# Weights of six stages of a four-layer network, requested during the normalisation ahead of each stage

## The chip, the cores and the metric

The kernel runs on one core of one Trainium2 chip. Its time is that of one execution on the device, in microseconds (us): the median of three runs was 2194.48 us (2192.84 to 2197.96). Before it is compared with after on the same measure.

## What is computed

The input is `x`, 2 sequences of 1024 tokens with 128 features, all float32. Four layers follow one another; each adds two residual branches, and each branch begins with a layer normalisation without scale or shift:

```python
x = x + L0_attn(layernorm(x))   # 16 heads of 64, causal softmax, two graph steps on the attention matrix, a linear map, projection, layernorm
x = x + L0_ffn(layernorm(x))    # 128 -> 512, a sine transform of the hidden values, relu, 512 -> 128
x = x + L1_attn(layernorm(x))   # one head of 64, causal softmax, projection
x = x + L1_ffn(layernorm(x))    # 8 experts of 128 x 128, each token takes the output of one
x = x + L2_attn(layernorm(x))   # 16 heads of 8, linear attention, gated
x = x + L2_ffn(layernorm(x))    # 8 experts, two per token, with a capacity
x = x + L3_attn(layernorm(x))   # state-space mixer: projection, convolution, scan over 16 states, projection
x = x + L3_ffn(layernorm(x))    # 8 experts, one per token
```

## The kernel before, in words

`x` stays in on-chip memory for the whole program, as `main_x` of 128 partitions by 16 tiles by 128 features. The program is a sequence of stages. Each stage opens a `scope` (lines 83 to 103), which hands out on-chip buffers, accumulator banks and semaphores, and then one block with a program for each engine. When a scope is left, GpSimd clears the scope's semaphores and all engines meet in a barrier (L89 in the profile). So no engine passes from one stage to the next before the slowest has ended its part, and a stage's buffers are free for the next stage.

Ahead of every branch stands `prenorm` (lines 106 to 169), a stage of its own. VectorE takes mean and variance of the 16 token tiles (L57, L60), ScalarE the square root (L145), VectorE five small steps and 16 normalised tiles `n_xn` (L132), TensorE turns each of them (L162), and ScalarE copies the turned tiles into `main_xnT`, 512 columns at a time (L148). The first layer runs this twice over (`rounds=2`). The last ScalarE copy ends the stage. SyncE has nothing to do in it, except where a router stands behind it: then the router's own small constants are requested there (L121).

Six branches request their weights at the start of their own stage, behind the barrier. SyncE issues the requests one after another, and the engines wait for a semaphore that counts all of them:

- `l0_attention` (prefix `l0a`): 13 requests of constants and masks (L302 to L309), eight of which wait until GpSimd has cleared three matrices (L331), since two blocks of 64 x 64 are put on the diagonal of each; then the first pair of heads' weights `wp` and `wvT` (L312, L313). VectorE makes four casts and constants (L780 to L783) before TensorE starts (L478, L483). It then runs 16 units, one for two heads of one sequence, with the next unit's weights requested inside the loop.
- `l0_ffn` (`l0f`): four requests (L982). VectorE prepares a small vector of angles (L951 to L955), GpSimd adds the output bias to all of `x` (L987), ScalarE takes a sine of the angles and then the hidden values (L1001), TensorE multiplies (L1083).
- `l1_attention` (`l1a`): five requests (L1136). TensorE makes queries, keys and values (L1189, L1195).
- `experts_dense` (`e`): the router `gate_top1` (`g`) with the normalisation inside it comes first; then three requests for each of the first two experts (L1446 to L1449), and those of the later experts inside the loop.
- `l2_attention` (`l2a`): seven requests (L1579). TensorE multiplies (L1594), VectorE adds a bias to each tile (L1672).
- `l3_mixer` (`mx`): eleven requests (L2439). TensorE projects (L2458), ScalarE copies (L2544), VectorE runs the four taps of the convolution (L2627, L2629).

The two branches with routed experts (`l2_moe`, `l3_moe`) already have their requests elsewhere and are not touched.

## Time and profile before

| | us |
|---|---|
| median of 3 runs | 2194.48 |
| profiled execution | 2188.13 |
| its span | 2186.3 |
| TensorE busy | 1659.2 |
| VectorE busy | 1128.1 |
| GpSimd busy | 785.5 |
| ScalarE busy | 679.5 |

The busy times are sums over the whole span. As the stages follow one another behind barriers, they say little about any one of them; the rows further down are read stage by stage. Times in those rows are us from the start of the span. PEclk is the granted clock of TensorE as a share of full speed: 1.00 is 2.4 GHz and 0.50 is 1.2 GHz.

### The profile page before, as it was taken

To read this page: it belongs to the slowest core of one execution; us is meant where nothing else is said; L and a number is where in the kernel's file an instruction comes from. 1 tells how busy PE (TensorE), PEld (TensorE's weight loads), DVE (VectorE), ACT (ScalarE), POOL (GpSimd) and SP (SyncE) were. 2 spreads that over 40 slices of the span, in tenths; PEclk is the share of its full clock that TensorE was granted. 3 is DMA by queue.
4 is the path that set the end of the run, shared out by engine and by line. 5 is a ranking of instruction groups with operands and counts; after the bars stand their busy time and mean duration, and the time that the engine had idled before them with its cause. 6 is when DMAs were issued, how large, how long until landed. Compare 5 with 4: busy or idle time off the path is not lost. (4 is left out here: it accounts for less than half of the span.)

```text
span 2186.3 us, 26512 instructions
## 1 busy us (share of the span) xinstructions
PE 1659.2 (76%) x9289; PEld 1028.0 (47%) x9289; DVE 1128.1 (52%) x2512; ACT 679.5 (31%) x990; POOL 785.5 (36%) x511
## 2 busy tenths in 40 slices
PE   3999999999989999999965576955209464767647
PEld 1555655555655556555642345624106211222437
DVE  4334443443444444444448823557703468999615
ACT  1333334433233333334303321322003154544212
POOL 0444345544244443455400031000152105899424
PEclk9899999999999999999886675977559676899759
DMA  1000000000000000000000000000511211212051
GB/s 42 6 6 6 5 5 5 5 0 5 6 1 5 5 5 5 5 5 0 1 1 11 0 6 3 18 12 2 178 46 33 57 31 57 78 67 78 3 153 67
DMA packets 47610, 55.87 MB, mean 26 GB/s; under 512 B 9296, under 2 KB 35048, under 8 KB 47264
## 3 DMA queue, kind: packets, MB, share of 16 engines
q1 hardware_dynamic: 44624, 48.91, 7.5%
q0 software_dynamic: 2912, 6.02, 0.8%
q8 instruction: 41, 0.67, 0.1%
q14 instruction: 33, 0.27, 0.0%
HBM read 42.75 MB, written 12.15 MB: 25 GB/s over the span
## 5 line engine op out<-in xcount | busy, mean ns | idle before, releaser
L356 POOL TENSOR_TENSOR l0a_acc<-l0a_E 128x1792 f32<-128x1792 f32 x16 | 64.3, 4018 | 448.0 <-ACT l0a_E L428 448.0
L821 DVE SCALAR_TENSOR_TENSOR l0a_scrap<-l0a_ring,main_ident 128x128 f32<-128x128 f32 x256 | 74.5, 291 | 271.7 <-PE l0a_ring L560 267.2
L428 ACT ACTIVATE l0a_E<-l0a_ring 128x1024 f32<-128x1024 f32 x192 | 148.8, 809 | 211.8 <-DVE l0a_scrap L821 210.6
L356 POOL TENSOR_TENSOR l0a_acc<-l0a_acc,l0a_E 128x1536 f32<-128x1536 f32 (+2 forms) x96 | 200.8, 2092 | 21.6 <-ACT l0a_E L428 14.0
L2505 PE MATMUL mx_ysum<-mx_hst,main_ident 128*128 128x512 f32 x256 | 142.6, 693 | 44.0 <-POOL mx_hst L2593 38.5
L2606 POOL TENSOR_TENSOR mx_dBu<-mx_XI,mx_BB 128x1024 f32<-128x1024 f32 x64 | 137.5, 2175 | 88.7 <-DVE mx_XI L2669 88.7
L570 PE MATMUL l0a_agg<-l0a_E,l0a_VH 128*64 128x512 f32 (+3 forms) x768 | 154.5, 510 | 0.0
L570 PE MATMUL l0a_agg<-l0a_E,l0a_F 128*64 128x512 f32 (+3 forms) x768 | 141.3, 496 | 0.0
L2578 ACT ACTIVATE mx_dA<-mx_DT,mx_A 128x512 f32<-128x512 f32 x128 | 87.9, 690 | 98.1 <-DVE mx_hst L2686 98.1
L2505 PEld LDWEIGHTS mx_ysum<-mx_hst,main_ident 128*128 128x128 f32 x256 | 54.1, 220 | 115.9 <-POOL mx_hst L2593 57.5
L162 PE MATMUL n_turned<-main_ident,n_xn 128*128 128x128 f32 x96 | 25.8, 458 | 90.6 <-DVE n_xn L132 90.6
L551 PE MATMUL l0a_ring<-l0a_QH,l0a_KH 64*128 64x512 f32 (+3 forms) x384 | 88.7, 459 | 5.5 <-ACT l0a_E L428 5.5
L2686 DVE TENSOR_TENSOR_SCAN mx_hst<-mx_dA,mx_hst,mx_dBu 128x512 f32<-128x512 f32 x64 | 82.1, 1283 | 7.9 <-DVE mx_hst L2686 1.0
L802 DVE TENSOR_REDUCE l0a_mx<-l0a_ring 128x2 fp32r<-128x1024 f32 x64 | 78.1, 1220 | 14.7 <-PE l0a_ring L501 14.5
L551 PEld LDWEIGHTS l0a_ring<-l0a_QH,l0a_KH 64*128 64x128 f32 x384 | 37.1, 190 | 92.0 <-ACT l0a_E L428 47.5
L2686 DVE TENSOR_TENSOR_SCAN mx_hst<-mx_dA,mx_dBu 128x512 f32<-128x512 f32 x64 | 77.4, 1209 | 2.5 <-POOL mx_dBu L2606 2.5
L501 PE MATMUL l0a_ring<-l0a_KH,l0a_QH 64*128 64x512 f32 (+3 forms) x384 | 70.2, 413 | 10.5 <-DVE l0a_KL L791 4.6
L483 PE MATMUL l0a_ring<-main_xnT,l0a_wp 128*128 128x512 f32 x128 | 78.1, 744 | 0.0
L628 PE MATMUL l0a_prod<-l0a_gnn,l0a_UT 128*128 128x128 f32 x512 | 75.8, 293 | 2.8 <-DVE l0a_S L848 0.9
L570 PEld LDWEIGHTS l0a_agg<-l0a_E,l0a_F 128*64 128x64 f32 x768 | 48.1, 136 | 62.4 <-issue 50.9
L401 ACT ACTIVATE l0a_top<-l0a_ring 64x1024 fp32r<-64x1024 f32 x16 | 16.3, 1017 | 189.9 <-PE l0a_ring L534 189.9
L628 PEld LDWEIGHTS l0a_prod<-l0a_gnn,l0a_UT 128*128 128x128 f32 x512 | 64.7, 198 | 15.4 <-issue 14.4
(483 smaller groups left out, 3701.2 us busy)
## 6 DMA issues: line engine op xcount, KB each, us to landing
mx_BB<-mx_brows SPq DMA_DIRECT2D x32, 512.0 KB, 3.6
me_W<-in_f_w SPq DMA_DIRECT2D x16, 256.0 KB, 9.6
l0a_wp<-in_wqkv SPq DMA_DIRECT2D x16, 192.0 KB, 2.3
moe_Wg<-in_f_wg SPq DMA_DIRECT2D x8, 256.0 KB
moe_Wu<-in_f_wu SPq DMA_DIRECT2D x8, 256.0 KB
moe_Wd<-in_f_wd SPq DMA_DIRECT2D x8, 256.0 KB
moe_Y<-rt_zeros SPq DMA_DIRECT2D x2, 1024.0 KB, 10.3
e_back<-moe_Y SPq DMA_DIRECT2D x8, 256.0 KB, 4.8
```

What stands on the lines that cost most here:

```text
L356: pool.tensor_tensor(dst, src, E[:, :, ecol[jt]:ecol[jt] + w], ALU.add).then_inc(acc_done, 1)
L428: act.activation(E[:, :, at:at + n], pair(k % 2)[:, :, 0:n], ACT.Exp).then_inc(exp_done, 1)
L483: mm = pe.matmul(half(dst, c), wp[:, part * P:(part + 1) * P], xnT[:, b * SEQ + c * 512:b * SEQ + (c + 1) * 512], start=True, stop=True)
L551: pe.matmul(out[:, h, 0:n], a[hi(h), keys], b[hi(h), at], start=a is KH and b is QH, stop=False, skip_group_check=True)
L570: mm = pe.matmul(agg[c][cols, lo - 512 * c:512], feats[:, jt, cols], E[:, h, at + lo:at + hi], start=(jt == 0), stop=(jt == 4 * c + 3 and ...
L628: mm = pe.matmul(prod[:, t * P:(t + 1) * P], UT[:, at:at + P], gnn[l][:, :], start=True, stop=True)
L802: dve.tensor_reduce(mx[:, :, it], pair(0)[:, :, :], AX_X, ALU.max).then_inc(max_done, 1)
L821: dve.scalar_tensor_tensor(scrap[:, :], pair(k % 2)[:, h, 0:P], 1.0, ident[:, :], ALU.mult, ALU.mult, accum_out=eii[:, jt, h:h + 1]).then_ ...
L2505: mm = pe.matmul(ysum[h][:, c * 512:(c + 1) * 512], ident[:, :], hst[:, k % DEEP, c * 512:(c + 1) * 512], start=(n == 0), stop=(n == NS - ...
L2578: act.activation(dA[:, c * 512:(c + 1) * 512], DT[:, h, b * SEQ + c * 512:b * SEQ + (c + 1) * 512], ACT.Exp, scale=A[:, h, n:n + 1]).then_ ...
L2606: pool.tensor_tensor(dBu[:, k % DEEP, :], du_of(h, b), BB[:, q % 3, :], ALU.mult).then_inc(dBu_ready, 1)
L2686: dve.tensor_tensor_scan(hst[:, k % DEEP, half], dA[:, half], dBu[:, k % DEEP, half], hst[:, k % DEEP, 511:512] if c else 0.0, ALU.mult, A ...
```

## The change

`prenorm` takes one more argument, `ahead`: a list of weights, each with the semaphore that counts their arrival. SyncE requests them at the start of the normalisation, behind the router's own constants where there are any. Each of the five stages that stand alone takes its weight buffers first, then calls the normalisation, and then takes its other buffers, so that the weights lie below the normalisation's buffers and outlive them. The wait counts in the stages stay in place.

```diff
-def prenorm(nc, name, x, xnT, ident, rounds=1, gamma=None, xn_keep=None, loads=(), gate=None):
+def prenorm(nc, name, x, xnT, ident, rounds=1, gamma=None, xn_keep=None, loads=(), gate=None, ahead=()):
...
             for dst, src in loads:
                 sp.dma_start(dst[:], src).then_inc(loaded, 16)
+            for weights, arrived in ahead:
+                for dst, src in weights:
+                    sp.dma_start(dst, src).then_inc(arrived, 16)
```

The feed-forward stage of the first layer shows the form that `l1_attention`, `l2_attention` and `l3_mixer` have too:

```diff
         b2 = sb("b2", [P, P])
+        w_in = sem("w_in")
+        norm([(((w1[:, :], d["f0_w1"]), (vec[:, :, :], d["f0_vec"]), (w2[:, :, :], d["f0_w2"]),
+                (b2[:, :], d["f0_b2"].partition_broadcast(P))), w_in)])
...
-        @block.sync
-        def _(sp):
-            for dst, src in ((w1, d["f0_w1"]), (vec, d["f0_vec"]), (w2, d["f0_w2"]), (b2, d["f0_b2"].partition_broadcast(P))):
-                sp.dma_start(dst[:], src).then_inc(w_in, 16)
```

In the first attention the three block-diagonal matrices come ready from memory in one buffer of 128 x 384, so three clears, the wait for them and six of the 13 requests go:

```diff
+        gnn_lin = sb("gnn_lin", [P, 3, P])
+        gnn, lin = [gnn_lin[:, l, :] for l in range(2)], gnn_lin[:, 2, :]
...
+        NCONST = 16 * len(consts)     # seven requests
+        norm([(((wp[:, 0:3 * P], d["wqkv"][0:P, :]), (wvT[:, :], d["wvT"][0:P, :])), w_in), (consts, const_in)])
...
-            for t in gnn + [lin]:
-                pool.memset(t[:, :], 0.0).then_inc(pool_step, 1)
             pool.memset(one[:, :], 1.0).then_inc(pool_step, 1)
-            pool.wait_ge(pool_step, 4)
+            pool.wait_ge(pool_step, 1)
```

The buffers and semaphores of the first two experts move into a scope of their own, which is opened before the router and left behind the experts, so that one more scope is left in the program:

```diff
+        with ExitStack() as held:
+            keys = (("f1_w1",), "f1_b1", "f1_w2")
+            weights, ahead = dense_weights(nc, held, "e1", d, keys)
             gate_top1(nc, "g1", d, ("f1_wg", ("f1_bg",), "f1_b2"), x, ident, pick,
-                      lambda loads, gate: prenorm(nc, "n3", x, xnT, ident, loads=loads, gate=gate))
-            experts_dense(nc, "e1", "gelu", d, (("f1_w1",), "f1_b1", "f1_w2"), x, xnT, pick)
+                      lambda loads, gate: prenorm(nc, "n3", x, xnT, ident, loads=loads, gate=gate, ahead=ahead))
+            experts_dense(nc, "e1", "gelu", d, keys, x, xnT, pick, weights)
```

`dense_weights` takes two buffers each for `up`, `down` and `b1` and the semaphores `w_in0` and `w_in1`, and lists the three transfers of experts 0 and 1; `load(0, 0)` and `load(1, 1)` at the start of `experts_dense` go.

## Rows read from the trace of the kernel before

**Rows 1.** Windows by stage: stretch, length, busy us of each engine, PEclk, DMA share, GB/s.
```profile
30.15:1141.70 1111.55, 1044.44 (x6752) 644.25 (x6752) 477.62 (x1124) 372.11 (x532) 451.51 (x276) 0.95 0.02 5
1722.00:1734.00 12.00, 4.19 (x16) 2.87 (x16) 9.68 (x54) 3.89 (x6) 0.00 (x0) 0.57 0.00 0
```
**Rows 2.** Timeline into `l0a`: start, us, engine, line, operation, count, [idle before, releaser].
```profile
30.15 0.33 SPq L302 DMA_DIRECT2D l0a_maskf<-in_cmask  x1
...
39.20 0.23 DVE L780 CAST l0a_mask<-l0a_maskf 128x128 bf16<-128x128 f32 x1 [11.08 <-DMA l0a_linb<-in_lin_b]
...
40.55 0.77 PE L478 MATMUL l0a_turn<-l0a_gnn,l0a_wvT 128*128 128x128 f32 x2 [11.90 <-DMA l0a_wvT<-in_wvT]
...
41.12 6.07 PE L483 MATMUL l0a_ring<-main_xnT,l0a_wp 128*128 128x512 f32 x8
```
**Rows 3.** Timeline into `l0f`.
```profile
1153.71 0.34 SPq L982 DMA_DIRECT2D l0f_w<-in_f_w  x1
...
1158.29 0.17 DVE L951 TENSOR_SCALAR l0f_room<-l0f_vec 128x4 f32<-128x4 f32 x1 [6.34 <-DMA l0f_b<-in_f_b]
...
1158.34 4.50 POOL L987 TENSOR_TENSOR main_x<-main_x,l0f_b 128x2048 f32<-128x2048 f32 x1 [62.74 <-DMA l0f_b<-in_f_b]
1158.50 4.36 DVE L952 TENSOR_SCALAR l0f_room<-l0f_room 128x4 f32<-128x4 f32 x1
```
**Rows 4.** Timeline into `l1a`.
```profile
1259.08 0.10 POOL L1140 MEMSET l1a_one<- 128x1 f32 x1 [96.24 <-POOLq L89]
...
1264.52 5.38 PE L1189 MATMUL l1a_ring<-main_xnT,l1a_wqkv 128*64 128x512 f32 x16 [6.82 <-DMA l1a_bout<-in_a_bout]
...
1268.24 1.02 ACT L1163 ACTIVATE l1a_QH<-l1a_ring 128x1024 fp32r<-128x1024 f32 x1 [9.91 <-PE l1a_ring L1189]
...
1269.95 1.02 ACT L1165 ACTIVATE l1a_KH<-l1a_ring 128x1024 fp32r<-128x1024 f32 x1 [0.69 <-PE l1a_ring L1189]
```
**Rows 5.** Timeline into the dense experts.
```profile
1364.50 0.33 SPq L1446 DMA_DIRECT2D e_up<-in_f_w  x1
...
1367.49 3.43 PE L1482 MATMUL e_hid<-main_xnT,e_up 128*128 128x512 f32 x4 [4.49 <-DMA e_b<-in_f_b]
```
**Rows 6.** Timeline into `l2a`.
```profile
1443.47 0.34 SPq L1579 DMA_DIRECT2D l2a_wkgv<-in_a_wkgv  x1
...
1449.46 4.49 PE L1594 MATMUL l2a_ring<-l2a_wkgv,main_xnT 128*128 128x384 f32 x8 [7.36 <-DMA l2a_bo<-in_a_bo]
...
1454.65 3.02 PE L1594 MATMUL l2a_ring<-l2a_wkgv,main_xnT 128*128 128x384 f32 x8
...
1458.30 0.69 DVE L1675 TENSOR_SCALAR l2a_room<-l2a_KGV 128x1024 f32<-128x1024 f32 x1
```
**Rows 7.** Timeline into the mixer.
```profile
1734.03 0.11 POOL L2588 MEMSET mx_XI<- 128x12 f32 x1 [25.78 <-POOLq L89]
...
1738.63 0.43 SPq L2439 DMA_DIRECT2D mx_sel<-in_sel  x1
...
1740.54 3.78 PE L2458 MATMUL mx_ysum<-main_xnT,mx_win 128*128 128x512 f32 x4 [7.89 <-DMA mx_sel<-in_sel]
...
1744.41 1.02 ACT L2544 ACTIVATE mx_XI<-mx_ysum 128x1024 f32<-128x1024 f32 x1 [11.13 <-PE mx_ysum L2458]
```
**Rows 8.** Windows of one us, TensorE alone: busy us (count), PEclk, DMA share, GB/s.
```profile
1151.00:1152.00 1.00, 1.00 (x5) 0.51 0.00 0
1152.00:1153.00 1.00, 0.33 (x2) 1.00 0.00 0
...
1155.00:1156.00 1.00, 0.00 (x0) 0.70 0.86 233
...
1344.00:1345.00 1.00, 1.00 (x7) 0.50 0.00 0
```
**Rows 9.** Timeline behind one scope (dense experts), then behind two (routed experts).
```profile
1431.36 3.19 DVE L57 BATCH_NORM_STATS2 n_n_stats<-main_x 128x6 f32<-128x128 f32 x16 [0.82 <-PEq L89]
1722.05 3.19 DVE L57 BATCH_NORM_STATS2 n_n_stats<-main_x 128x6 f32<-128x128 f32 x16 [1.35 <-PEq L89]
```

More of the change, by code:

```diff
@@ L472, in _ @@
             pe.wait_ge(cast_done, 4)
-            pe.wait_ge(pool_step, 4)
+            pe.wait_ge(pool_step, 1)
             def composite(u):
@@ L1130, in l1_attention @@
         block = ctx.enter_context(nc.Block(no_gpsimd_drain=True))
-        @block.sync
-        def _(sp):
-            for dst, src in ((wqkv[:, :], d["a1_qkv"]), (maskf[:, :], d["cmask"]), (wout[0:DI, :], d["a1_out"]),
-                             (wout[DI:2 * DI, :], d["a1_out"]), (bout[:, :], d["a1_bout"].partition_broadcast(P))):
-                sp.dma_start(dst, src).then_inc(w_in, 16)
         @block.gpsimd
@@ L1417, in _, with dense_weights, experts_dense @@
                 dve.tensor_tensor(s, bb[g % 2][:, :, :], s, ALU.add).then_inc(bb_added, 1)
-def experts_dense(nc, name, kind, d, keys, x, xnT, cw):
+def dense_weights(nc, ctx, name, d, keys):
+    upkeys, b1key, downkey = keys
+    F = d[upkeys[0]].shape[1]
+    FC = F // P
+    sb, pb, sem = scope(nc, ctx, name + "w")
+    up = [[sb(f"up{j}_{u}", [P, F]) for u in range(len(upkeys))] for j in range(2)]
+    down = [sb(f"down{j}", [P, FC, P]) for j in range(2)]
+    b1 = [sb(f"b1_{j}", [P, FC]) for j in range(2)]
+    w_in = [sem("w_in0"), sem("w_in1")]
+    ahead = []
+    for e in range(2):
+        rows = slice(e * P, (e + 1) * P)
+        first = [(up[e][u][:, :], d[k][rows, :]) for u, k in enumerate(upkeys)]
+        first += [(down[e][:, :, :].rearrange("p a b -> p (a b)"), d[downkey][rows, :])]
+        if b1key is not None:
+            first += [(b1[e][:, :], d[b1key][rows, :])]
+        ahead += [(first, w_in[e])]
+    return (up, down, b1, w_in), ahead
+def experts_dense(nc, name, kind, d, keys, x, xnT, cw, held):
     upkeys, b1key, downkey = keys
@@ L1427, in experts_dense @@
         sb, pb, sem = scope(nc, ctx, name)
-        up = [[sb(f"up{j}_{u}", [P, F]) for u in range(NU)] for j in range(2)]
-        down = [sb(f"down{j}", [P, FC, P]) for j in range(2)]
-        b1 = [sb(f"b1_{j}", [P, FC]) for j in range(2)]
+        up, down, b1, w_in = held
         a = sb("a", [P, 2, FC, 512])
@@ L2390, in l3_mixer @@
         sel1 = sb("sel1", [96, 2 * NS])
+        w_in = sem("w_in")
+        loads = ((win, "m_win"), (conv, "m_conv3"), (convb, "m_convb"), (wdt8, "m_wx_dt"), (wbc, "m_wx_bc"), (wdt, "m_wdt"),
+                 (bdt, "m_bdt"), (A, "m_alog3"), (Dp, "m_D"), (wout, "m_wout"), (sel1, "sel32"))
+        NW = 16 * len(loads)
+        norm([([(dst[:], d[k]) for dst, k in loads], w_in)])
         sel = sb("sel", [96, NS, P], BF16)
@@ L2437, in _ @@
         def _(sp):
-            for dst, k in loads:
-                sp.dma_start(dst[:], d[k]).then_inc(w_in, 16)
             sp.wait_ge(brow_kept, NB)
@@ L2716, in more_layouts @@
     out["gnn_row"] = np.concatenate([a["L0_attn_gnn_b"], a["L0_attn_gnn_b"]], 1)
+    gnn_lin = np.zeros((P, 3, P), np.float32)
+    for h in range(2):
+        r = slice(h * DH, (h + 1) * DH)
+        gnn_lin[r, 0, r], gnn_lin[r, 1, r], gnn_lin[r, 2, r] = *a["L0_attn_gnn_w"], a["L0_attn_lin_w"]
+    out["gnn_lin"], out["linb2"] = gnn_lin, np.tile(a["L0_attn_lin_b"].reshape(DH, 1), (2, 1))
     out["f0_w1"], out["f0_w2"] = a["L0_ffn_W1"], chunks(a["L0_ffn_W2"])
```

92 lines of the change are left out of this document (36 added, 56 removed).

## The prediction

> **What bounds the kernel now.** I read the page's chain of waits first and found it of little use: followed back from the last instruction it ends inside the last expert stage, at 2093 us. So I cut the span into stages, at the first instruction behind each barrier, and looked at each by itself. The first attention alone takes 1111.55 us with TensorE busy for 1044.44 of them; a normalisation of the usual kind takes 12.00 us, in which SyncE issues nothing [rows 1]. The change touches neither the inside of a stage nor the inside of a normalisation. It touches the seams, and there I read the timeline. At each of six seams the reader is to see one pattern: SyncE's first request comes as the stage opens, then all engines stand still, and the first instruction of TensorE and VectorE is released by the landing of the last request [rows 2 to 7]. As every stage ends in a barrier of all engines, what such a seam loses is lost to the end of the program, and what it gains is gained there. So the forecast is a sum over seams.
>
> **The wait that goes, seam by seam.** In each the price is the start of the first work now, less the moment at which the stage's first instruction that waits for nothing starts, which is where that work can start when the data are there. VectorE follows SyncE or GpSimd within about 0.1 us, which I allow.
>
> First attention: the stage opens at 30.15 and TensorE starts at 40.55 [rows 2]. The four casts on VectorE then come first; now they run from 39.20 to about 39.8, well inside the wait, and afterwards they stand in front of TensorE: 30.15 + 0.15 (the clear of `one`) + 0.7 = 31.0. Gain 9.55. The three clears that go lie beside the wait already and give nothing of their own. The six requests that go are part of the 10 us of issue and landing, and are not counted twice.
>
> First feed-forward: VectorE starts at 1158.29 against 1153.71 for the opening, 4.58 [rows 3]. But this stage does not begin with TensorE. VectorE's second small step, 4 columns wide, took 4.36 us and ended when GpSimd's addition over all of `x` ended (1158.34 + 4.50 = 1162.84; 1158.50 + 4.36 = 1162.86). The addition begins with the stage in both kernels, so the stall moves with it and stays. GpSimd's first instruction is what opens the second attention and the mixer [rows 4, 7], so it is as early out of the barrier as any engine, and may now catch the first small step instead of the second, which puts one step of 0.17 us behind the stall. Gain 4.58 - 0.28 = 4.3. Were GpSimd late enough for the small steps to pass, the 4.36 us would go as well; I don't expect it.
>
> Second attention: 1264.52 against 1259.08, less 0.14 for the start: 5.3 [rows 4]. Dense experts: 1367.49 against 1364.50, less 0.1: 2.9 [rows 5]. Third attention: 1449.46 against 1443.47, less 0.1: 5.9 [rows 6]. Mixer: 1740.54 against 1734.03, less 0.1: 6.4 [rows 7]. Together 9.55 + 4.3 + 5.3 + 2.9 + 5.9 + 6.4 = 34.35.
>
> **What hides the requests now.** They pass to SyncE's queue in the normalisation. The longest list is the mixer's: eleven requests, the last at 1738.63, 4.6 us behind the first, and everything landed at 1740.5, so 6.5 us in all [rows 7]. The normalisation ahead of it lasts 12.00 us [rows 1], with nothing else on SyncE or the DMA queues, so 5.5 us are to spare there, and more elsewhere. In the router the new requests stand behind the router's own four, so these are not delayed. The transfers write into buffers that no engine uses at that time. I cost all of this at nothing; if the cover failed at the mixer the loss would be what the landing is late, and never more than the 6.4 us of that seam. The block-diagonal matrices now bring 192 KB with their zeros, against 96 KB in six pieces, under a normalisation twice as long as the others.
>
> **What is added.** One more scope is left, behind the dense experts: its clear and its barrier. The trace shows no such thing alone, but behind one scope VectorE resumes after 0.82 us of idleness, and behind the two nested scopes of the routed experts after 1.35 [rows 9]. The difference, 0.5, is my value; nothing and 1.35 are the ends. The order in which semaphores are handed out changes too, which could split a clear in two; that lies within these ends.
>
> **TensorE's clock at the seams.** The turning of the tiles finds TensorE at half clock (1.2 GHz) and raises it as it ends: PEclk is 0.51 for the us before 1152 and 1.00 in the next, with no work behind it, and falls back within the us from 1155 [rows 8]. Now the stage's first matmul comes at 1158 or later and starts at the low level every time. Afterwards it comes some 1.4 us behind the last turn, while the clock is high, and TensorE is then at work. What that is worth is taken from rows at either level. In the second attention the queries' eight matmuls took 3.72 us up to ScalarE's start (1264.52 to 1268.24, low), the keys' eight took 1.71 (1268.24 to 1269.95, high) [rows 4]; with 0.2 us of latency, 1.8. In the mixer four matmuls take 3.87 us up to ScalarE [rows 7], at the high level half of the 3.4 us of work: 1.7, and VectorE's taps, which set the pace there, wait for that copy. In the third attention the first half took 5.19 us (1449.46 to 1454.65, mostly low), the second 3.65 (1454.65 to 1458.30) [rows 6]; 1.3 of the difference I count, since VectorE is near its own pace. In the first attention eight matmuls took 6.07 us [rows 2]; eight at the high level would take what the mixer's four of the same shape took at the low one, 3.78 [rows 7]: 2.3 at most, and I take half, 1.2, as no row says that the clock was raised before them. In the first feed-forward GpSimd's stall hides TensorE, and in the dense experts the turns and routing end at a low clock (0.50 at 1344 to 1345 [rows 8]): nothing in both. Sum 1.8 + 1.7 + 1.3 + 1.2 = 6.0. The ends: nothing, or even 2 us lost where a fall comes at a worse moment inside the stage; and 12 us, if the first attention keeps the high level through its first unit as well.
>
> The rows show that the clock rises during turns. The Trainium skill, "TensorE: Matmul & The Clock Gate", Part 4, states the contrary, that the full clock does not engage for transposes, as they don't count as TensorE work in the same way. By that rule the first matmuls would start low as before and this term would be zero; by the rows it is 6.0.
>
> **Sum.** 34.35 + 6.0 - 0.5 = 39.85 us. Made against the profiled execution's own time (2188.13, its span 2186.3 and 1.8 around it): 2148.3. The median of the runs shown is 6.35 above that execution, and I expect the new median to stand against it: 2194.48 - 39.85 = 2154.6.
>
> **Rivals.**
>
> 1. The high clock is not kept: some 1.4 us of idleness remain between the last turn and the first matmul, and it may fall as it does now, within the us from 1155 [rows 8]. Against it: before, TensorE had nothing at all to do from the last turn until then, and now it has 1.5 us of matmuls in that stretch. The gain is then 34.35 - 0.5, about 34, and the time is 2160.6.
> 2. More than the sum comes: the first attention keeps its clock through the values' matmuls, or VectorE passes GpSimd in the first feed-forward (4.36). Some 46 to 48 us: 2147.
> 3. The change doesn't do what it says: a transfer is late or the engines find something else to wait for as the stage opens, such as their own instructions, whose loading is now hidden under the wait. Against it: the normalisations and the router open without any wait for data, and VectorE resumes after 0.82 to 1.35 us there [rows 9]. If half of the seams' waiting came back as such a wait, 17 us less: 2171.
> 4. Slower than before: the first attention is TensorE's, and its granted clock is 0.95 [rows 1]. That share depends on how the dips, one in each unit, fall, and the unit now starts at another moment. At level 0.50 the work of a stretch takes twice as long. If TensorE bounds all of that stage, it needs 1111.55 x 0.95 = 1056 us of full clock; at a mean of 0.917 that takes 1152 us, 40 more than now, which is the point from which the whole gain is gone, and at 0.91 it takes 1160, 49 more, and the time is 2203. Against it: there are 16 units, each with its own order of waits, and the three runs before lie within 0.23% of each other, so the share does not hang on one start.
>
> **Chances.** Forecast 0.55, rival 1 0.24, rival 2 0.14, rival 3 0.04, rival 4 0.03. The range 2144 to 2164 takes in the forecast, both clock cases and the run-to-run spread of 2 to 3 us; it leaves out the last two. A difference under 0.2% (4.4 us) could not be told from none. Faster 0.95, same 0.02, slower 0.03.
>
> **What would show it.** In the new profile SyncE's requests of weights stand beside the statistics (L57) of each normalisation; the first matmul of each of the six stages follows the last copy of the turned tiles by about 1 us, 1.6 in the first attention, and no DMA is its releaser; the first matmuls of 512 columns are issued every 0.43 us, not every 0.85; the small step of 4.4 us is still there in the first feed-forward; the gap behind the dense experts is about 1.3 us. A stage whose length from first matmul to barrier has grown, or a PEclk under 0.94 in the first attention, would prove me wrong.

## The result: 2156.32 us, where 2154.6 was forecast

| | before | after |
|---|---|---|
| median | 2194.07 (4 runs) | 2156.32 (4 runs, 2155.75 to 2157.74) |
| profiled execution | 2188.13 | 2155.89 |
| its span | 2186.3 | 2154.2 |
| TensorE busy | 1659.2 | 1655.9 |
| VectorE busy | 1128.1 | 1130.6 |
| GpSimd busy | 785.5 | 784.9 |
| ScalarE busy | 679.5 | 679.8 |

The ratio is 0.9826, with a 95% interval of 0.9809 to 0.9843. No engine does notably less work; what went is waiting. The changed kernel was run in two more series beside the kernel before: 2159.53 against 2189.58 (0.9852, 0.9836 to 0.9868) and 2159.91 against 2194.72 (0.9841, 0.9816 to 0.9865). The gains of the three series are 37.8, 30.1 and 34.8 us, 34.2 on the mean, and their intervals overlap. The first one alone would have flattered the forecast's 39.85.

### The profile page after: what moved, and what is told of

Its sections match the earlier page's. It is cut to its first block and busy times, and to the rows that moved or that the text cites. A ratio compares the mean times of both kernels' runs of the same rounds, so it can differ in the third digit from the quotient of the medians.

```text
span 2154.2 us, 26516 instructions
## 1 busy us (share of the span) xinstructions
PE 1655.9 (77%) x9289; PEld 1028.1 (48%) x9289; DVE 1130.6 (52%) x2512; ACT 679.8 (32%) x990; POOL 784.9 (36%) x508
## 3 DMA queue, kind: packets, MB, share of 16 engines
HBM read 42.85 MB, written 12.15 MB: 26 GB/s over the span
## 5 line engine op out<-in xcount | busy, mean ns | idle before, releaser
L2608 POOL TENSOR_TENSOR mx_dBu<-mx_XI,mx_BB 128x1024 f32<-128x1024 f32 x64 | 137.6, 2178 | 85.5 <-DVE mx_XI L2671 85.5
L543 PEld LDWEIGHTS l0a_ring<-l0a_QH,l0a_KH 64*128 64x128 f32 x384 | 36.9, 189 | 91.8 <-ACT l0a_E L420 47.5
L562 PEld LDWEIGHTS l0a_agg<-l0a_E,l0a_F 128*64 128x64 f32 x768 | 48.1, 136 | 62.4 <-issue 50.9
L620 PE MATMUL l0a_prod<-l0a_gnn_lin,l0a_UT 128*128 128x128 f32 x512 | 75.6, 292 | 2.8 <-DVE l0a_S L840 0.9
L475 PE MATMUL l0a_ring<-main_xnT,l0a_wp 128*128 128x512 f32 x128 | 73.6, 706 | 0.0
L620 PEld LDWEIGHTS l0a_prod<-l0a_gnn_lin,l0a_UT 128*128 128x128 f32 x512 | 64.4, 198 | 15.1 <-issue 14.2
```

The costliest lines, as they stand in the source:

```text
L475: mm = pe.matmul(half(dst, c), wp[:, part * P:(part + 1) * P], xnT[:, b * SEQ + c * 512:b * SEQ + (c + 1) * 512], start=True, stop=True)
L543: pe.matmul(out[:, h, 0:n], a[hi(h), keys], b[hi(h), at], start=a is KH and b is QH, stop=False, skip_group_check=True)
L562: mm = pe.matmul(agg[c][cols, lo - 512 * c:512], feats[:, jt, cols], E[:, h, at + lo:at + hi], start=(jt == 0), stop=(jt == 4 * c + 3 and ...
L620: mm = pe.matmul(prod[:, t * P:(t + 1) * P], UT[:, at:at + P], gnn[l][:, :], start=True, stop=True)
L2608: pool.tensor_tensor(dBu[:, k % DEEP, :], du_of(h, b), BB[:, q % 3, :], ALU.mult).then_inc(dBu_ready, 1)
```

## The profile after

The seams first, in the order of [rows 2 to 7]. The timeline of the changed kernel (start, us, engine, line, operation, count, idle before and releaser):

```profile
7.77 0.33 SPq L124 DMA_DIRECT2D l0a_wp<-in_wqkv  x1
7.80 0.68 DVE L57 BATCH_NORM_STATS2 n_n_stats<-main_x 128x6 f32<-128x128 f32 x3 [7.80 <-PEq L2778]
...
30.11 0.10 POOL L324 MEMSET l0a_one<- 128x1 f32 x1 [29.58 <-POOLq L89]
30.32 0.23 DVE L772 CAST l0a_mask<-l0a_maskf 128x128 bf16<-128x128 f32 x1 [2.09 <-POOL l0a_one L324]
...
31.05 0.46 PE L470 MATMUL l0a_turn<-l0a_gnn_lin,l0a_wvT 128*128 128x128 f32 x2 [2.44 <-DVE l0a_part L775]
31.35 5.30 PE L475 MATMUL l0a_ring<-main_xnT,l0a_wp 128*128 128x512 f32 x8
...
1139.39 4.50 POOL L977 TENSOR_TENSOR main_x<-main_x,l0f_b 128x2048 f32<-128x2048 f32 x1 [58.15 <-POOLq L89]
1139.41 1.96 PE L1073 MATMUL l0f_hid<-main_xnT,l0f_w 128*128 128x512 f32 x4 [1.43 <-PEq L89]
1139.80 4.11 DVE L943 TENSOR_SCALAR l0f_room<-l0f_vec 128x4 f32<-128x4 f32 x1 [2.21 <-PEq L89]
...
1240.30 5.19 PE L1177 MATMUL l1a_ring<-main_xnT,l1a_wqkv 128*64 128x512 f32 x16 [1.42 <-PEq L89]
...
1243.81 1.02 ACT L1151 ACTIVATE l1a_QH<-l1a_ring 128x1024 fp32r<-128x1024 f32 x1 [4.30 <-PE l1a_ring L1177]
...
1340.07 1.19 PE L1486 MATMUL e_hid<-main_xnT,e1w_up 128*128 128x512 f32 x1 [1.55 <-PEq L89]
...
1405.08 0.29 DVE L57 BATCH_NORM_STATS2 n_n_stats<-main_x 128x6 f32<-128x128 f32 x1 [1.23 <-PEq L89]
...
1417.23 4.65 PE L1596 MATMUL l2a_ring<-l2a_wkgv,main_xnT 128*128 128x384 f32 x8 [1.42 <-PEq L89]
...
1697.11 0.43 SPq L124 DMA_DIRECT2D mx_sel<-in_sel  x1
...
1705.22 3.75 PE L2460 MATMUL mx_ysum<-main_xnT,mx_win 128*128 128x512 f32 x4 [1.79 <-PEq L89]
...
1709.06 1.02 ACT L2546 ACTIVATE mx_XI<-mx_ysum 128x1024 f32<-128x1024 f32 x1 [5.00 <-PE mx_ysum L2460]
```

The reader is to look at the releasers. Where [rows 2 to 7] had a DMA in front of each stage's first work, there is now the barrier (L89), or, in the first attention, VectorE's own small casts (L772 to L775). SyncE's requests (L124) stand beside the statistics; the last of the mixer's is issued at 1697.11, eight us ahead of its use. The small step of 4 columns still takes 4.11 us beside GpSimd's addition over all of `x`.

So that every seam can be priced, I cut each trace at the first instruction of each normalisation (L57) and then at the first work of the stage behind it: TensorE's first matmul, or ScalarE's first hidden values in the first feed-forward. "Seam" is the time between the two, "body" what follows until the next normalisation. In us, for two profiles of the kernel before and three of the changed one (one from each series):

| | before | before, again | after | after, again | after, third |
|---|---|---|---|---|---|
| `l0a` seam | 32.85 | 32.80 | 23.25 | 23.39 | 23.33 |
| `l0f` seam | 22.15 | 22.09 | 17.76 | 17.90 | 17.91 |
| `l1a` seam | 17.58 | 17.34 | 12.17 | 12.16 | 12.16 |
| dense experts seam | 39.02 | 39.03 | 36.09 | 36.08 | 36.07 |
| `l2a` seam | 18.10 | 17.84 | 12.15 | 12.15 | 12.16 |
| mixer seam | 18.49 | 18.48 | 12.53 | 12.51 | 12.52 |
| `l0a` body | 1101.2 | 1101.1 | 1096.3 | 1107.2 | 1095.5 |
| dense experts body | 63.87 | 63.88 | 65.01 | 65.12 | 65.11 |
| `l2_moe`, whole | 208.95 | 208.63 | 211.42 | 211.64 | 208.76 |
| mixer body | 316.10 | 320.50 | 320.11 | 319.86 | 319.07 |
| `l3_moe`, whole | 129.62 | 134.14 | 128.84 | 129.44 | 130.66 |

The other bodies agree within 0.5 us (`l0f` 83, `l1a` 64, `l2a` 64). Before to after the seams give 9.60 + 4.39 + 5.41 + 2.93 + 5.95 + 5.96 = 34.24 us. The spans differ by 32.1, since the bodies moved too: -4.9 in the first attention, +1.1 in the dense experts, +2.5 in the routed experts `l2_moe`, +4.0 in the mixer, -0.8 in `l3_moe`, +0.2 in all the rest. Whether these movements belong to the change or to the execution is what the experiments had to show as well.

## Experiments

### The changed kernel and the kernel before, once more

The changed kernel unaltered, in two series:

> The changed kernel once more, unaltered, timed against the kernel before. My account is that the six seams give 34.2 us in every execution (9.6 + 4.4 + 5.4 + 2.9 + 6.0 + 6.0, read from the two profiles) less 0.4 for the extra scope, and that the rest of the difference of medians (37.75) is where TensorE's clock happens to rise and fall. It expects a ratio of 0.982 to 0.985, the same six starts in the new profile within 0.1 us each, counted from the start of the normalisation, but a clock that rises during the turns in other normalisations than last time (then in the first two, and not in those ahead of the second and third attention and the mixer). The rival, that the clock term of the forecast is real and only this profile missed it, expects the first matmuls behind the turns at the high level in at least three of the four seams.

> The changed kernel once more, unaltered, as a third profile of it and beside the others of this call. By the ledger of the first two: normalisation starts and seams the same within 0.2 us, the first attention behind its first matmul 1096 or 1107 us, the routed experts 211.4 to 211.7, the mixer behind its first matmul 320. If the routed experts take 211.5 again while before_warm2 or before show 209, the 2.6 us there belong to the change; if they take 208.6, as in port, they are the execution's. Time 2156 to 2160, 0.9826 to 0.985 of before.

And the kernel before, unaltered:

> The kernel before, unaltered, for a second profile. Behind the first matmul of each stage three profiles of the changed kernel form agree with one another and not with the one profile of before: the mixer takes 319.8 to 320.1 us against 316.1, the routed experts of the third layer 211.4 to 211.7 against 209.0, the dense experts 65.0 to 65.1 against 63.9. If these 7.6 us are a lasting cost of the change, the second profile of before has 316, 209 and 63.9 again. If they only depend on where the clock falls in one execution, at least one of the three comes out as in the changed kernel. The first attention behind its first matmul differed by up to 13 us between profiles of one kernel and is expected anywhere from 1094 to 1108.

Measured: 2159.53 (2154.93 to 2169.3), 2159.91 (2155.02 to 2166.04), and for the kernel before 2196.18 in one run; the table above has their ledgers. The seams repeat within 0.15 us, but for 0.26 at `l1a` and `l2a` before. The bodies do not: the first attention takes 1107.2 in one profile of the changed kernel and 1095.5 in another; the routed experts (`l2_moe`) 211.6 and 208.8; in the kernel before the mixer takes 316.1 and 320.5, and `l3_moe` 129.6 and 134.1. So neither the 2.5 us of the routed experts nor the 4 us of the mixer is shown to be a lasting cost of the change. Only the 1.1 us of the dense experts are the same in every profile.

What sets the first attention's body shows in the stage's windows. Columns: stretch, length, busy us of TensorE, its weight loads, VectorE, ScalarE and GpSimd, PEclk, DMA share, GB/s. After, then after again:

```profile
31.05:1127.39 1096.34, 1037.15 (x6752) 641.04 (x6752) 479.69 (x1120) 372.00 (x532) 450.92 (x272) 0.96 0.01 4
```
```profile
31.20:1138.37 1107.17, 1050.66 (x6752) 647.00 (x6752) 475.94 (x1121) 372.19 (x532) 451.20 (x272) 0.95 0.01 4
```

The same 6752 matmuls are busy for 13.5 us more and the stage is 10.8 us longer, with the other engines as before. The records of the granted clock hold 92 us at the low level in the first and 115 in the second, 94.6 in the third profile (body 1095.5), 111 in the kernel before again (1101.1) and 118.4 in the kernel `late` below (1108.3).

One thing has to be known when PEclk is read: the record can miss a low stretch. The first matmuls of this stage, in the profile after again:

```profile
31.75 6.11 PE L475 MATMUL l0a_ring<-main_xnT,l0a_wp 128*128 128x512 f32 x8
```
```profile
32.00:33.00 1.00, 1.00 (x2) 1.00 0.00 0
```

The record says 1.00, but the matmuls of 512 columns start 0.85 us apart, the pace at the low level, and only the last 0.43. The first profile of the kernel before has the same, PEclk 1.00 and starts 0.85 us apart, from 41.12 [rows 2], for about 5 us. Both counts of the low level (115 here, 105.8 in the kernel before) are some 5 us short by it; with them the kernel before has 111 in both profiles, and the same body. So a PEclk of 1.00 at a stage's opening is believed here only where the matmuls' pace says the same.

The routed experts vary with their time at the low clock as the first attention does. TensorE alone (busy us and count, PEclk, DMA share, GB/s), 133 to 137 us into the stage, after and then third, whose stages start within 0.2 us of each other:

```profile
1614.00:1615.00 1.00, 0.22 (x2) 0.50 0.03 8
1617.00:1618.00 1.00, 1.00 (x3) 0.50 0.00 0
```
```profile
1614.00:1615.00 1.00, 1.00 (x5) 1.00 0.00 0
1617.00:1618.00 1.00, 1.00 (x5) 1.00 0.00 0
```

One low spell, which begins 35 us into the stage in both, ends at 137.6 us in the one and at 130.8 in the other. That goes with the 2.7 us. What decides where it ends these runs don't show.

### Requests at the end of the normalisation

If the gain is the wait for the landing, requests that are made only when the last tile is normalised must give most of it back.

```diff
+            if ahead:
+                sp.wait_ge(xn_ready, TT)
             for weights, arrived in ahead:
```

> The requests stay in the normalisations, but SyncE issues them only when VectorE has made the 16th normalised tile, some 1.8 us before the stage opens. If the gain is the landing that is hidden, it comes back as far as the landing is late: counted from that tile, requests and landing take 4.6 us in the first feed-forward, 5.3 in the second attention, 6.0 in the third, 6.5 in the mixer, about 6.4 with the casts behind in the first attention, so these five start later by 2.8 + 3.4 + 4.1 + 4.2 + 4.2 = 18.7 us than in the changed kernel, and the dense experts, which have the router in between, by nothing: about 2175 us. A rival under which the gain comes from the shorter program of the first stage, or from where the buffers lie, expects about 2156 to 2158.

Measured: 2177.23 (2172.68 to 2183.36), ratio 0.9938 (0.9922 to 0.9954), 17.7 us above the changed kernel of the same series, where 18.7 was expected. Against the profile after again the first works come later by 5.2 (`l0a`), 2.7, 3.6, 0.0 (dense experts), 4.1 and 4.0 (mixer), 19.6 in all. The timeline at the first feed-forward has the wait back, with its old releaser:

```profile
1156.13 0.43 SPq L126 DMA_DIRECT2D l0f_b<-in_f_b  x1
...
1159.55 0.17 DVE L945 TENSOR_SCALAR l0f_room<-l0f_vec 128x4 f32<-128x4 f32 x1 [4.78 <-DMA l0f_b<-in_f_b]
...
1159.76 4.37 DVE L946 TENSOR_SCALAR l0f_room<-l0f_room 128x4 f32<-128x4 f32 x1
```

Buffers, semaphores and requests are those of the changed kernel; only the moment differs. So it is the landing, and no effect of the new placement. The dense experts lose nothing, as the router's work behind the normalisation still covers their requests.

### Is it the place or the number of requests, in the first attention?

The change makes two edits there: 13 requests become seven (beside the two of the first weights) with no clear ahead of them, and all nine are made early. Here they are nine, made at the start of the stage.

```diff
-        norm([(((wp[:, 0:3 * P], ...), (wvT[:, :], ...)), w_in), (consts, const_in)])
+        own = [(((wp[:, 0:3 * P], ...), (wvT[:, :], ...)), w_in), (consts, const_in)]
+        norm([])
...
+            for todo, arrived in own:
+                for dst, src in todo:
+                    sp.dma_start(dst, src).then_inc(arrived, 16)
```

> The first attention alone requests its nine transfers behind the barrier again (ready-made block-diagonal matrices, no clears); the other five stages stay as changed. Nine requests take 4.1 us to issue and the last lands 2.2 us later, then come 0.7 us of casts: TensorE starts at about 36.9 instead of 31.05. Expected 5.8 us more than the changed kernel, 2162, and of the 9.6 us of this seam 3.7 are then due to fewer requests and no clears, 5.9 to the place of the requests. If the 4.9 us that the first attention gained in the two profiles beyond its seam belong to the earlier start, they go too: 2167.

Measured: 2163.90 (2161.47 to 2169.54), ratio 0.9886 (0.9868 to 0.9904), 4.4 us above the changed kernel. The stage's timeline:

```profile
30.25 0.33 SPq L309 DMA_DIRECT2D l0a_wp<-in_wqkv  x1
...
33.94 0.43 SPq L309 DMA_DIRECT2D l0a_linb<-in_linb  x1
37.74 0.23 DVE L777 CAST l0a_mask<-l0a_maskf 128x128 bf16<-128x128 f32 x1 [9.51 <-DMA l0a_linb<-in_linb]
...
38.47 0.77 PE L475 MATMUL l0a_turn<-l0a_gnn_lin,l0a_wvT 128*128 128x128 f32 x2 [9.72 <-DVE l0a_part L780]
```

The first matmul starts 30.67 us behind the normalisation's start, 7.3 later than with early requests and 2.1 earlier than in the kernel before. So of the seam's 9.6 us the place is worth 7.3 to 7.4 and the fewer requests (with ready-made matrices) about 2.2. Expected were 5.9 and 3.7, and a first matmul at 36.9 that came at 38.47: VectorE's first cast comes 3.4 us behind the end of the last request, not 2.2. The median shows less than 7.3, with a body of 1094.0 in this profile against 1107.2. That is the variation of the body again, and medians of four runs don't average it out.

### Making TensorE busy before the turns

If the clock at the seams matters, it can be raised on purpose: seven matmuls of 512 columns on `ident` and `x`, whose result the turns overwrite. In `warm` there are 18 of them in the first layer's double normalisation too, behind the first root; in `warm2` that normalisation is left alone.

```diff
+            for n in range(0 if rounds > 1 else 7):
+                pe.matmul(bank[3][:, :, :].rearrange("p a b -> p (a b)"), ident[:, :],
+                          x[:, 0:4, :].rearrange("p a b -> p (a b)"), start=True, stop=True)
             for g in range(4):
                 for j in range(4):
                     pe.wait_ge(xn_ready, 4 * g + j + 1)
```

> Added to the changed kernel: in each normalisation TensorE multiplies 7 times 128x512 (18 times in the first, behind the first square root) before the first turn, into a bank that the fourth group of turns overwrites; the products are not used. They take 3 to 6 us in a stretch of 6.4 us in which TensorE has nothing to do, so they cost nothing themselves. If the clock carries over from the turns into the stage, the first matmuls of the second and third attention and the mixer run at the high level: 1.8 + 1.3 + 1.7 us less, and up to 2 in the first attention, so about 2150. If the 1.4 us without work at the seam are enough to lose it, as in the first attention of the changed kernel where it fell 0.7 us after the first matmul, the time is that of the changed kernel, 2156.

Measured: 2151.19 (2142.0 to 2154.88), ratio 0.9809 (0.9788 to 0.9829), mean clock 0.867 to 0.871 where the changed kernel has 0.846 to 0.856; 8.3 us under the changed kernel. The first attention's seam grew by 4.5 us, as 18 matmuls were too many there. The gain came inside, against the profile after again: router 2.7, routed experts (`l2_moe`) 5.4, mixer 4.7, `l3_moe` 5.7. Part of the last three is the execution's; the last is 129.2 to 129.4 in `warm2` and `best2`, as in the changed kernel. But at 205.1 to 206.2 us in this kernel, `warm2` and `best2` `l2_moe` is below every profile of the changed kernel (208.8 to 211.6).

> As the variant with extra matmuls ahead of the turns, but without those of the first normalisation, which delayed its turns by 4.6 us there. The other gains of that variant were not at the seams, where the clock fell again in the gap (low from 0.2 us before to 3.3 us behind the first matmul of the second attention), but behind them: router 2.7, routed experts 5.3, mixer 4.8, last stage about 4.5. These are expected again, with the 4.6 us on top: 14 to 18 us less than the changed kernel. If the last run owed its 8 us to the luck of its clock, the gain stays under 6.

Measured: 2149.28 (2142.07 to 2156.78), ratio 0.9803 (0.9777 to 0.9829). The changed kernel did not run in this series; by its ratios in the others (0.9826 to 0.9852) this is 5 to 11 us less than it would take, not the 14 to 18 that were expected. The first attention's seam is back at 23.41.

The same seven matmuls in the kernel before, with nothing else changed:

> The kernel before, with warm2's seven matmuls in the same normalisations and nothing else. It tells whether warm2's gain has to do with the early requests. Theory now held: it has not. The matmuls gain inside the stages behind (the router by 2.75 us, the routed experts by 5 to 6, the mixer by about 4), where TensorE finds its clock raised or its falls elsewhere, whatever is requested when; and they gain nothing at the seams, as the clock falls again at the first gap. Then this kernel takes 7 to 10 us less than before: about 2185 (2182 to 2188), with every seam as long as before. Rival, the prediction's idea: the clock raised in the normalisation is carried to the first matmuls only where these follow at once; with the old wait of 3 to 6 us between them it is lost, and the gain is that of the router alone, 3 us at most: 2189 to 2192.

Measured: 2190.24 (2186.61 to 2196.23, 12 runs), ratio 0.9981 (0.9966 to 0.9996), 4.5 us less than before. The expectation fails, and its rival too: 4.5 lies between 3 and 7, and by the interval it may be anything from 0.9 to 7.5. In the profile the router's seam is 2.5 us shorter; the other seams lie within 0.4 us of the kernel before, and `l2_moe` takes 208.82. One row shows what the late requests do to a clock that has been raised. TensorE alone, after the last turn ahead of the second attention, whose first matmul starts at 1264.96:

```profile
1258.00:1259.00 1.00, 0.35 (x2) 1.00 0.00 0
1259.00:1260.00 1.00, 0.00 (x0) 1.00 0.00 0
1260.00:1261.00 1.00, 0.00 (x0) 1.00 0.13 27
```

The records of the clock put its fall at 1262.1, into the wait for the landing; it stays low until 4.0 us behind the first matmul.

### Work for TensorE in the mixer's gap

The mixer's body took 4 us more in the changed kernel than in the first profile before, and its long stretch at the low clock begins ahead of the projections of the step sizes. Five matmuls of 512 columns, whose result is not used, are put there to keep the clock high.

```diff
+            pe.wait_ge(dbl_kept, 1)
+            for n in range(5):
+                pe.matmul(work[1][:, 0:512], ident[:, :], xnT[:, 0:512], start=True, stop=True)
```

> Five extra matmuls of 128x512 on TensorE in the mixer, ahead of the projections of the step sizes, into a bank that is free there and overwritten after; the products are not used. In the changed kernel the clock falls just as these projections begin (43.3 us behind the stage's first matmul) and all run at the low level, 1.056 us each; in before and in two of the variants the first half still runs high. If this is the mixer's 4 us, the extra work keeps the clock, half or all of the projections run at 0.59 us, and the stage falls from 332.5 to 328 or 329 us. If the 4 us come from elsewhere, the extra work costs 0 to 2 us and the stage stays at 332 to 334.

Measured: 2167.84 (2159.52 to 2172.45), ratio 0.9871 (0.9839 to 0.9903). The mixer with its normalisation took 332.85 us, against 332.64, 332.37 and 331.59 in the changed kernel: nothing gained. The long low spell began 50.9 us behind the first matmul, not 43, and ended at 95.3 (101.4 and 93.9 in profiles of the changed kernel). That is 44 us at the low level against 58 in the first profile after, with the same body (320.3 and 320.1). So this spell is not what the mixer's 4 us are made of, and their cause stays open.

### GpSimd's addition in the first feed-forward

The prediction left the 4.4 us stall of a small VectorE step in place. If GpSimd's addition causes it, it must go with the addition. Here TensorE adds the bias as a product of a row of ones and `b2`, which makes GpSimd's work one clear of 0.2 us.

```diff
-            pool.wait_ge(w_in, 64)
-            pool.tensor_tensor(x[:, :, :], x[:, :, :], b2[:, :].unsqueeze(1).broadcast_to([P, TT, P]), ALU.add)
+            pool.memset(ones[:, :], 1.0).then_inc(bias_added, 1)
...
+                for t in range(4):
+                    mm = pe.matmul(outp[g % 2][:, t, :], ones[0:1, :], b2[0:1, :], start=False, stop=True,
+                                   skip_group_check=True)
```

> In the first feed-forward the output bias is no longer added to x by GpSimd as the stage opens; TensorE adds it as a product of a row of ones with the bias row behind each group of the down projection (16 small matmuls in all). If GpSimd's 4.5 us addition is what makes VectorE's first small step take 4.1 us, that step takes 0.2 us and the stage's first hidden values come 4.1 us sooner: about 4 us less than the changed kernel, the stage 96.7 us instead of 100.7 between the normalisations. If the small step is slow for a reason of its own, nothing changes.

Measured: 2156.58 (2153.65 to 2171.98), ratio 0.9847 (0.9809 to 0.9886). The step takes 0.17 us and the first hidden values come 14.54 us behind the normalisation's start, not 17.76. The cause of the stall is shown: it is the addition. But the stage took 106.01 us against 100.74. The timeline shows the step, and where the time went:

```profile
1139.86 0.17 DVE L943 TENSOR_SCALAR l0f_room<-l0f_vec 128x4 f32<-128x4 f32 x1 [2.35 <-PEq L89]
...
1166.04 2.07 PE L1065 MATMUL l0f_outp<-l0f_w,l0f_a 128*128 128x128 f32 x8 [2.55 <-ACT l0f_a L1001]
1168.04 2.07 PE L1068 MATMUL l0f_outp<-l0f_b,l0f_ones 1*128 1x128 f32 x8
1170.04 2.93 PE L1075 MATMUL l0f_hid<-main_xnT,l0f_w 128*128 128x512 f32 x3
```

A bias row of one partition costs TensorE as much as a product over 128 (2.07 us for eight passes), and it stands in front of the next group's hidden values, for which the other engines wait. Four groups make 8.3 us. So the passes were moved to the head of the group (`start=(t == 0)` on the bias, `start=False` on the products), where TensorE waits for ScalarE anyway:

> The changed kernel with the bias of the first feed-forward added on TensorE, as in port, but with the eight ones-row passes of each group of 512 tokens at the head of the group's products instead of at their end. In port they took 2.07 us at the end of each of four groups, 8.3 us in all, and TensorE, which works in order, came to the next hidden values that much later: the stage took 106.01 us against 100.74, though its first hidden value came 3.2 us earlier. At the head of the group they lie where TensorE waits for the next activated values (2.5 to 3.5 us of idleness between two chunks), so they should cost nothing. If that is what made port slower, the stage takes 100.74 - 3.2 = 97.5 us (97 to 98.5) and the kernel gains about 3 us on the changed one. Rival: the group's place in TensorE's order matters and only part of the 8.3 us is hidden; then the stage takes 99 to 103. Second rival: the ones-row passes lower the granted clock in the stage, and it stays near 106.

Measured: 2155.28 (2147.06 to 2162.38), ratio 0.9811 (0.9784 to 0.9838). The medians can't tell it from the changed kernel, 2159.91 in that series. The stage can: 97.09 us, 3.65 to 4.0 less than in the three profiles of the changed kernel, and 97.5 was expected. In the timeline of this kernel the bias goes first, and the next products wait for ScalarE as before:

```profile
1160.93 2.07 PE L1063 MATMUL l0f_outp<-l0f_b,l0f_ones 1*128 1x128 f32 x8
...
1167.38 2.07 PE L1068 MATMUL l0f_outp<-l0f_w,l0f_a 128*128 128x128 f32 x8 [0.67 <-ACT l0f_a L1001]
```

### Both together

> port2 and warm2 together: the changed kernel with the bias on TensorE at the head of each group, and with seven matmuls of 512 columns (their result is overwritten by the turns) at the start of TensorE's part of each normalisation but the first layer's double ones. If the two gains add, warm2's (2149.28 against 2156 to 2159 for the changed kernel, 7 to 10 us) and port2's (3 us): 2146 (2142 to 2150), and the lowest of the series. Rival: where the granted clock falls in the first attention and in the mixer decides, and differs from one execution to the next by 4 to 11 us within one kernel, so that the 3 us of the stage can't be told from warm2's result (2149).

Measured: 2143.35 (2141.43 to 2145.62, 5 runs), ratio 0.9762 (0.9738 to 0.9786). It is the lowest of the study, and 16.6 us under the changed kernel of its series. The two gains taken singly, by medians some 8 and 4.6 us, are known to a few us only, so that they do more than add is not shown. This kernel also shows a seam at which the high clock is kept, at the second attention. Its timeline, and TensorE's windows:

```profile
1239.14 3.65 PE L1183 MATMUL l1a_ring<-main_xnT,l1a_wqkv 128*64 128x512 f32 x16 [1.42 <-PEq L89]
1241.12 1.02 ACT L1157 ACTIVATE l1a_QH<-l1a_ring 128x1024 fp32r<-128x1024 f32 x1 [2.76 <-PE l1a_ring L1183]
```
```profile
1238.50:1239.00 0.50, 0.00 (x0) 1.00 0.00 0
1239.00:1239.50 0.50, 0.36 (x2) 1.00 0.00 0
...
1242.00:1242.50 0.50, 0.50 (x4) 1.00 0.00 0
```

The queries' copy starts 1.98 us after the first matmul, where it takes 3.51 to 3.72 in the three profiles of the changed kernel; the stage with its normalisation takes 74.13 us, against 75.85 to 76.30.

## Why the prediction was right, and which term was not

**The seams: right.** 34.35 was forecast and 34.24 measured. One by one, forecast and measured: first attention 9.55 and 9.60, feed-forward 4.3 and 4.39, second attention 5.3 and 5.41, dense experts 2.9 and 2.93, third attention 5.9 and 5.95, mixer 6.4 and 5.96. The mixer is the one that fell short, by 0.44. Its opening moved: from the normalisation's last copy to the stage's first instruction it is 1.11 us (1704.07 to 1705.18), against 0.74 before (1733.28 to 1734.02). The forecast took that time as fixed.

**The cover: right.** The mixer's eleven requests end with the one at 1697.11, and no first work has a DMA as its releaser. `late` shows the price of the cover where it is taken away, 19.6 us, and none in the dense experts.

**GpSimd's stall: right.** It moved to the first small step, as the prediction said it might, and it is the addition that makes it (`port`).

**The extra scope: right.** The gap behind the dense experts is 1.23 us, against 0.82 [rows 9]: 0.41 lost where 0.5 was forecast.

**The dense experts' body: not foreseen.** It is 1.1 us longer in all three profiles (65.0 to 65.1 against 63.9). 0.41 of it is the scope's gap. The rest is the clock, which rose 3.0 us behind the first matmul before and 5.8 us behind it after: the stage began 2.9 us earlier, the rise did not. The first eight products of `e_outp` stood at either side of it, before and after:

```profile
1371.68 1.16 PE L1492 MATMUL e_outp<-e_down,e_a 128*128 128x128 f32 x8 [0.76 <-ACT e_a L1513]
```
```profile
1344.23 1.91 PE L1496 MATMUL e_outp<-e1w_down,e_a 128*128 128x128 f32 x8 [0.41 <-ACT e_a L1517]
```

**The clock at the seams: the step that failed.** The forecast was that the stage's first matmuls would find the clock raised by the turns, 6.0 us in all. It took the rise from one seam, the first feed-forward's [rows 8]. The kernel before has it at more than that one: in both of its profiles the record puts the rise within 0.4 us of the end of the last turn at the feed-forward, the second and third attention and the mixer. At the second attention, where the last turn ends at 1257.70 (TensorE alone):

```profile
1256.50:1257.00 0.50, 0.50 (x4) 0.50 0.00 0
1257.50:1258.00 0.50, 0.20 (x1) 0.70 0.00 0
1258.00:1258.50 0.50, 0.00 (x0) 1.00 0.00 0
```

What failed is that the rise would stay with the turns when everything ahead of them moved. In the changed kernel it is there at the feed-forward in one profile of three, and at the second attention the first shows this (last turns, gap, first matmuls, and the rise):

```profile
1238.00:1238.50 0.50, 0.50 (x4) 0.50 0.00 0
1239.00:1239.50 0.50, 0.00 (x0) 0.50 0.00 0
1240.00:1240.50 0.50, 0.20 (x2) 0.50 0.00 0
1243.00:1243.50 0.50, 0.50 (x4) 0.56 0.00 0
1243.50:1244.00 0.50, 0.50 (x4) 1.00 0.00 0
```

Here the turns did not raise the clock, so there was nothing to keep. The low spell began 10.5 us ahead of the first matmul (9.9 in the other two profiles), inside the normalisation, and outlasted the turns; before, it began 9.6 us ahead of the normalisation. Over the three profiles of the changed kernel the first matmuls ran high at one of the nine seams of `l1a`, `l2a` and mixer: the mixer of the third.

```profile
1701.00:1702.00 1.00, 0.00 (x0) 0.96 0.00 0
1702.00:1703.00 1.00, 0.24 (x1) 1.00 0.00 0
...
1702.76 1.96 PE L2460 MATMUL mx_ysum<-main_xnT,mx_win 128*128 128x512 f32 x4 [1.79 <-PEq L89]
1704.81 1.02 ACT L2546 ACTIVATE mx_XI<-mx_ysum 128x1024 f32<-128x1024 f32 x1 [3.20 <-PE mx_ysum L2460]
```

There ScalarE starts 2.05 us behind the first matmul, against 3.84 in the first profile after: 1.8, where 1.7 was forecast for the mixer. So the price of a kept clock at the opening was right, and how often it is kept was wrong: on the mean of the three profiles 0.6 us in the mixer and 0.5 in the first attention (eight matmuls in 5.30 us instead of 6.07 in two of them), about 1 us instead of 6.0. What the prediction cites of the Trainium skill, "TensorE: Matmul & The Clock Gate", Part 4, that the full clock does not engage for transposes, agrees with eight of these nine seams; the trace disagrees at the ninth (PEclk 1.00 at 1702), and in the kernel before at the first feed-forward [rows 8] and the second attention (1.00 at 1258). Whether the turns of this kernel are run in the mode that the page speaks of, the trace does not say.

Of the 1.8 us in the mixer not all reaches the end of the stage: with its normalisation it takes 331.59 us in that profile, 0.8 to 1.05 less than in the other two. At the second attention it does: 74.02 us in `warm2` and 74.13 in `best2`, 1.7 to 2.3 less than in the changed kernel, where 1.8 was forecast.

What it takes for a high clock to reach the stage is seen in the kernels with the seven matmuls, where it is high during the turns at all of these seams. With late requests (`before_warm2`) it falls during the wait, and the second attention, the third and the mixer open at the low pace. With early requests (`warm`, `warm2`, `best2`) the second attention opens at the high pace in two kernels of three, the mixer in two of three and for half of its opening in the other (ScalarE 2.05, 2.05 and 2.91 us behind the first matmul), the third attention in none: there the clock falls within 0.12 us of the first matmul. So its term of 1.3 was never tested. The mixer also opens high in `third`, `port` and `port2`, without such matmuls.

The seven matmuls take 4.5 us off the kernel before, and 8 to 12 off the changed one (`warm` against after again 8.3, `best2` against `port2` 11.9). That is no proof that the early requests make them worth more: the intervals of these differences are some 3 to 8 us wide to each side, and in the profiles most of the surplus lies in `l2_moe` (205.1 to 206.2 us against 208.8), whose own requests are the same in all of these kernels.

**The sum.** 34.24 - 0.41 - 0.7 (the dense experts' clock) + 1 is about 34.1, and the three series gave 34.2 on the mean. An agreement to 0.1 us is luck too, as each series is known to 3.5 us or more and the bodies of the first attention, the mixer and `l3_moe` move by 4 to 12 us. That is the first rival (34 us, 2160.6), except that the clock was mostly not raised, rather than raised and lost. The forecast of 2154.6 came within 1.7 us of 2156.32 by luck: the first series happened to gain 3.6 us more than the mean of the three, which covered most of the 5 us of clock that did not come.

**Its own signs of being wrong.** Two of them showed. At five of the six openings of the second attention and the mixer, the first matmuls of 512 columns started some 0.85 us apart, not 0.43. And the dense experts grew from first matmul to barrier, in every profile.

**The other rivals.** VectorE did not pass GpSimd in the first feed-forward (rival 2). Nothing took the place of the waits: the seams came out whole but for the 0.44 us of the mixer (rival 3). The granted clock of the first attention stayed at 0.95 to 0.96 (rival 4), and its body's variation, 1095.5 to 1107.2, is the largest term that the prediction did not carry: it is wider than the whole clock term. The 2 to 3 us that it allowed from run to run were too few as well: single runs of the kernel before lie between 2185.1 and 2205.1 us.

**What stays open.** Why the same turns raise the clock at four seams in both profiles of the kernel before and mostly not in the changed one, what ends the long low spells in the routed experts and the mixer, and what makes the mixer take 315 to 320 us behind its first matmul.

## What to carry to other kernels

A wait for data at the opening of a stage, between barriers, can be priced from the trace: first work less the first instruction that waits for nothing. Here that held to 0.1 us at five seams and to 0.44 at the sixth, and the wait comes off whole if the stage ahead covers issue and landing. A gain from a raised clock is real, but where the clock rises in the old kernel says little of the new one, in which the work ahead has moved: it is no term of a sum until the new kernel's trace shows it, at every seam and in more than one execution. And an operation of TensorE that is small in data is not small in its queue: move it to where the engine waits anyway.

## What the runs showed of the hardware

- The record of the granted clock can miss a low stretch: in seven of the 14 profiles PEclk reads 1.00 somewhere in the first 45 us while matmuls of 512 columns start 0.85 us apart instead of 0.43. Wherever else such matmuls follow one another without a gap, record and pace agree.
- One kernel's first attention differs by 11.7 us between executions, with the same 6752 matmuls, as the time at the low clock differs. Medians of this kernel that lie 5 us apart can hardly be told from each other (`port2`); the table by stage repeats within 0.3 us at the seams.
- A bias as a matmul over one partition, 128 columns wide, takes as long as one over 128 partitions: 2.07 us for eight passes, both. The Trainium skill, "TensorE: Matmul & The Clock Gate", "Why this matters for your kernels", states the same of 32 partitions; the trace extends it to one.
- A VectorE step of 4 columns took 4.11 us while GpSimd added over 128 x 2048, and 0.17 us without it, although the two work on different buffers. The Trainium skill, "SBUF — State Buffer", "SBUF: two separate sides", states that VectorE and GpSimd can hold a shared pair of ports by an exclusive lock, for a whole instruction; the blocked step, 4.11 us beside an addition of 4.50, agrees.
